# A three-part decoder layer on one core: row totals of both norms summed by VectorE's additions, squares about the mean summed by ScalarE

## What is computed

```
def _layernorm(x, axis=-1, eps=1e-05):
    m = jnp.mean(x, axis=axis, keepdims=True)
    v = jnp.var(x, axis=axis, keepdims=True)
    return (x - m) / jnp.sqrt(v + eps)
...
    x = _layernorm(x + _L0_attn_ref(x, ...), axis=-1)
    x = _layernorm(x + _L0_xattn_ref(ctx_1024, x, ...), axis=-1)
    x = _layernorm(x + _L0_ffn_ref(x, ...), axis=-1)
    return x
```

## Time and profile before

| | |
|---|---|
| runs | 1366.23 us median of 3 (1363.86 to 1369.6) |
| the profiled execution | 1370.82 us, of which the span of the instructions is 1368.9 us |
| PE busy | 1144.9 us (84%) |
| DVE busy | 1100.1 us (80%) |
| POOL busy | 997.2 us (73%) |
| ACT busy | 852.6 us (62%) |
| mean granted clock of PE | 0.88 of full speed |
| first scan, last scan | 51.95 us, 756.3 us |
| experts' first load of the slot table lands | about 820 us |

### The profile page before, as it was taken

How to read it: one execution, slowest core, us unless ns; L and a number is a source line. 1 busy time by engine, 2 the same in 40 slices (tenths; PEclk the granted TensorE clock), 3 DMA queues, 4 the chain that set the end, 5 groups by cost and what they waited for, 6 DMA issues and landing times. The chain is left out here.

```text
span 1368.9 us, 19497 instructions
## 1 busy us (share of the span) xinstructions
PE 1144.9 (84%) x6481; PEld 768.9 (56%) x6481; DVE 1100.1 (80%) x1534; ACT 852.6 (62%) x1536; POOL 997.2 (73%) x788
## 2 busy tenths in 40 slices
PE   7489997898968889978987536999999999999950
PEld 2234433353324544333533326999899999999950
DVE  2379988989968699778899354988889888989946
ACT  5474584734855445756354225888888888888843
POOL 0778778867999887999989703777777777777744
PEclk9688997899979689977998557999999999999985
DMA  6535326322252412163131208999999999999978
GB/s 239 136 74 193 103 64 154 108 56 72 49 139 57 129 51 64 34 152 108 31 81 32 62 17 277 267 305 303 308 301 303 307 307 307 303 314 304 302 130 331
DMA packets 97491, 235.26 MB, mean 172 GB/s; under 512 B 20705, under 2 KB 21217, under 8 KB 96753
## 3 DMA queue, kind: packets, MB, share of 16 engines
q1 hardware_dynamic: 65648, 162.66, 39.1%
q0 software_dynamic: 31744, 71.37, 21.8%
HBM read 147.48 MB, written 52.94 MB: 146 GB/s over the span
## 5 line engine op out<-in xcount | busy, mean ns | idle before, releaser
L1189 DVE TENSOR_TENSOR_SCAN hst<-hst,dbu 128x512 f32<-128x512 f32 x256 | 299.2, 1214 | 98.8 <-POOL dbu L1005 72.9
L1005 POOL TENSOR_TENSOR dbu<-rep,bc 128x1024 f32<-128x1024 f32 x128 | 301.8, 2359 | 67.1 <-PE y_ps L377 36.1
L1600 POOL DMA_INDIRECT sum_rows<-ye,tokens x128 | 205.5, 1605 | 101.0 <-ACT ye L1679 73.9
L377 PE MATMUL y_ps<-dbu,cs 128*32 128x512 f32 x512 | 158.0, 701 | 74.7 <-DVE dbu L1195 63.5
L1592 POOL DMA_INDIRECT xe<-x_rows,tokens x128 | 148.9, 1163 | 83.6 <-issue 37.8
L771 ACT ACTIVATE hst<-rep,small_sb 128x512 f32<-128x512 f32 x256 | 165.9, 685 | 47.7 <-DVE dbu L1195 42.1
L415 PE MATMUL ring<-wqkv,xT 128*128 128x512 f32 x384 | 178.7, 609 | 0.3 <-DVE x2T L1277 0.2
L1195 DVE TENSOR_TENSOR dbu<-hst,bc 128x1024 f32<-128x1024 f32 x128 | 156.7, 1225 | 4.4
L1642 PE MATMUL low<-xh,w1h 128*128 128x256 f32 x512 | 150.8, 295 | 0.7 <-DVE w1l L1753 0.7
L1642 PE MATMUL low<-xl,w1h 128*128 128x256 f32 x512 | 145.6, 284 | 0.0
L1642 PE MATMUL low<-xh,w1l 128*128 128x256 f32 x512 | 145.5, 284 | 0.0
(11 more groups left out here) (190 smaller groups left out, 2705.6 us busy)
## 6 DMA issues: line engine op xcount, KB each, us to landing
w<-in_gate_up SPq DMA_DIRECT2D x64, 768.0 KB
rep<-made SPq DMA_DIRECT2D x256, 128.0 KB
w<-in_down SPq DMA_DIRECT2D x64, 256.0 KB
bc<-bc_rows SPq DMA_DIRECT2D x64, 128.0 KB, 2.9
w<-in_down SPq DMA_DIRECT2D x64, 128.0 KB
rows<-sum_rows SPq DMA_DIRECT2D x16, 512.0 KB, 9.3
sum_rows<-x2T SPq DMA_DIRECT2D x1, 4608.0 KB, 16.7
xT<-in_x_turned SPq DMA_DIRECT2D x16, 256.0 KB, 3.0
```

The costliest lines, as they stand in the source:

```text
L377: ins = pe.matmul(y_ps[rows, :], sel, dbu[:, n % WORK, g, :], start=(k == 0), stop=(k == QUADS - 1))
L1005: pool.tensor_tensor(dbu[:, n % WORK, :, :], rep[:, i % 2, :, 1, :], bc[:, k, 0, :].unsqueeze(1).broadcast_to([P, 2, T]), ALU.mult).then_i ...
L1189: dve.tensor_tensor_scan(h, h, dbu[:, n % WORK, i, :], 0.0, ALU.mult, ALU.add).then_inc(scanned, 1)
L1600: pool.indirect_dma_start(sum_dram[e % SUMS], bass.IndirectOffsetOnAxis(ap=tokens[:, e, j:j + 1], axis=0), ye[:, e % YE, j, :], None, comp ...
```

## The change

Means and variances of both norms are no longer made with bn_stats and bn_aggr.

- DVE's addition, `scalar_tensor_tensor`, writes the row totals beside its result (total, total2). The second sum was a `tensor_tensor` and is now a `scalar_tensor_tensor` with a factor of 1.
- ACT has a new `center(t)`: the total times -1/512, which is the negative mean, and after a wait for it a Square of x1 with that as bias, whose row sums go to power. Its full output goes to a buffer that nobody reads. `center(t)` stands after decays(n + 8), ahead of the last excess or steps and of qT and kT. `center2(b, j)` does it for x2, four in a row, in tile c = 0 between taking v and decays(n + 8), and in the tail.
- POOL's roots take power times 1/512, plus eps; shift is the negative mean times rstd. `last_root` has one operation less. `norm_root(t - 1)` moves from k = 0, behind the first dbu product, to k = 1, behind everything that is done there.

```diff
+            def center(t):
+                c = t % NT
+                taken(act, f"wo{t}")
+                act.activation(total[:, c:c + 1], total[:, c:c + 1], ACT.Copy, scale=-1.0 / D).then_inc(centered, 1)
+                act.wait_ge(centered, t + 1)
+                act.activation(square_out[:, :], x1[:, c, :], ACT.Square, bias=total[:, c:c + 1],
+                               accum_out=power[:, c:c + 1]).then_inc(stats_ready, 1)
+
+            def center2(b, j):
+                taken(act, f"yT{b}_{j}")
+                act.activation(total2[:, j:j + 1], total2[:, j:j + 1], ACT.Copy, scale=-1.0 / D).then_inc(centered2, 1)
+                act.wait_ge(centered2, NT * b + j + 1)
+                act.activation(square_out[:, :], x2[:, j, :], ACT.Square, bias=total2[:, j:j + 1],
+                               accum_out=power2[:, j:j + 1]).then_inc(stats2_ready, 1)
...
+                    if back and c == 0:
+                        for j in range(NT):
+                            center2(b - 1, j)
                     if more:
                         decays(n + 8)
+                    center(t)
...
             def norm_root(t):
                 c = slice(t % NT, t % NT + 1)
                 pool.wait_ge(stats_ready, t + 1)
-                root(rstd[:, c], mv[:, t % NT, 1:2])
-                pool.tensor_scalar(shift[:, c], mv[:, t % NT, 0:1], rstd[:, c], -1.0, ALU.mult, ALU.mult).then_inc(rstd_ready, 1)
+                root(rstd[:, c], power[:, c], scale=1.0 / D)
+                pool.tensor_tensor(shift[:, c], total[:, c], rstd[:, c], ALU.mult).then_inc(rstd_ready, 1)
...
-                        if k == 0 and t:
-                            norm_root(t - 1)
...
                         if k in (3, 4) and c == 1:
                             steps_of_u(b, k - 1)
+                        if k == 1 and t:
+                            norm_root(t - 1)
...
                 dve.scalar_tensor_tensor(out=x1[:, c, :], in0=full(dve, f"wo{t}")[:, :], scalar=rms[:, c:c + 1],
-                                         in1=x_in[:, t % 2, :], op0=ALU.mult, op1=ALU.add).then_inc(drain_sem(f"wo{t}"), 1)
-                taken(dve, f"wo{t}")
-                own.step(dve.bn_stats(st[:, c, :], x1[:, c, :]))
-                own.settle()
-                dve.bn_aggr(mv[:, c, :], st[:, c, :]).then_inc(stats_ready, 1)
-                assert own.n == NORM_STEPS
+                                         in1=x_in[:, t % 2, :], op0=ALU.mult, op1=ALU.add,
+                                         accum_out=total[:, c:c + 1]).then_inc(drain_sem(f"wo{t}"), 1)
...
-                dve.tensor_tensor(x2[:, j, :], full(dve, use)[:, :], x1[:, j, :], ALU.add).then_inc(drain_sem(use), 1)
-                taken(dve, use)
-                own.step(dve.bn_stats(st2[:, j, :], x2[:, j, :]))
...
+                dve.scalar_tensor_tensor(out=x2[:, j, :], in0=full(dve, use)[:, :], scalar=1.0, in1=x1[:, j, :],
+                                         op0=ALU.mult, op1=ALU.add, accum_out=total2[:, j:j + 1]).then_inc(drain_sem(use), 1)
```

More of the change, by code:

```diff
@@ L84 @@
 TURN_STEPS = 3
-NORM_STEPS = 1
-NORM2_STEPS = NT
 ROUTE_STEPS = 25
@@ L186, in mixers @@
         rms = sb("rms", [P, NT])
-        st = sb("st", [P, NT, 6])
-        mv = sb("mv", [P, NT, 2])
+        total = sb("total", [P, NT])
+        power = sb("power", [P, NT])
+        square_out = sb("square_out", [P, D], F16)
         rstd = sb("rstd", [P, NT])
         shift = sb("shift1", [P, NT])
-        st2 = sb("st2", [P, NT, 6])
-        mv2 = sb("mv2", [P, NT, 2])
+        total2 = sb("total2", [P, NT])
+        power2 = sb("power2", [P, NT])
         rstd2 = sb("rstd2", [P, NT])
@@ L277, in mixers @@
         squared = sem("squared")
-        norm_steps = sem("norm_steps")
+        centered = sem("centered")
+        centered2 = sem("centered2")
         x1_ready = sem("x1_ready")
@@ L982, in _ @@
             gate_z(B - 1, 3)
+            for j in range(NT):
+                center2(B - 1, j)
             second_norm(B - 1)
@@ L1029, in _, with root @@
             roots = Chain(pool, root_steps)
-            def root(dst, src, done=None):
-                roots.step(pool.tensor_scalar(dst, src, 1.0, EPS, ALU.mult, ALU.add))
+            def root(dst, src, done=None, scale=1.0):
+                roots.step(pool.tensor_scalar(dst, src, scale, EPS, ALU.mult, ALU.add))
                 roots.settle()
@@ L1047, in norm_root @@
                 pool.wait_ge(stats_ready, t + 1)
-                root(rstd[:, c], mv[:, t % NT, 1:2])
-                pool.tensor_scalar(shift[:, c], mv[:, t % NT, 0:1], rstd[:, c], -1.0, ALU.mult, ALU.mult).then_inc(rstd_ready, 1)
+                root(rstd[:, c], power[:, c], scale=1.0 / D)
+                pool.tensor_tensor(shift[:, c], total[:, c], rstd[:, c], ALU.mult).then_inc(rstd_ready, 1)
             def last_root(b):
                 pool.wait_ge(stats2_ready, NT * (b + 1))
-                roots.step(pool.tensor_scalar(shift2[:, :], mv2[:, :, 0], -1.0, None, ALU.mult))
-                root(rstd2[:, :], mv2[:, :, 1])
-                pool.tensor_tensor(shift2[:, :], shift2[:, :], rstd2[:, :], ALU.mult).then_inc(rstd2_ready, 1)
+                root(rstd2[:, :], power2[:, :], scale=1.0 / D)
+                pool.tensor_tensor(shift2[:, :], total2[:, :], rstd2[:, :], ALU.mult).then_inc(rstd2_ready, 1)
             def rotate(t):
@@ L1418, in _ @@
                     if back and c == 0:
-                        second_sum(b - 1, chain["norm"], 2)
-                        second_sum(b - 1, chain["norm"], 3)
+                        second_sum(b - 1, 2)
+                        second_sum(b - 1, 3)
                     if front:
@@ L1425, in _ @@
                     add_attention(t)
-                    if back and c == 0:
-                        second_stats(b - 1, chain["norm"])
                     if back and c == 1:
```

18 lines of the change are left out of this document (4 added, 14 removed).

## The result

| | kernel before | changed kernel |
|---|---|---|
| median of the runs | 1365.55 us (6 runs, 1363.55 to 1369.6) | 1377.76 us (6 runs, 1374.64 to 1381.67) |
| ratio, 95% interval | | 1.0083 [1.0062, 1.0105] |
| profiled execution | 1370.82 us, span 1368.9 | 1380.38 us, span 1378.5 |
| first scan, last scan | 51.95, 756.32 us | 48.80, 768.67 us |

The change makes the kernel 0.83% slower, 11.3 us [8.5, 14.3]. The forecast was slower by 6.1 us. In the profiled executions the changed kernel takes 719.9 us from the first scan to the last instead of 704.4; what stands ahead is 3.1 us shorter and what stands behind 2.8. Both differ by as much between executions of kernels that are the same there (over the 14 profiled executions of this document the first scan starts at 48.80 to 51.95 us). So the loss is in the mixers, and single profiled executions give its size only roughly.

What follows compares the result with a forecast made beforehand. No engine bounds the mixers all the way; TensorE, DVE, and waits for ACT or POOL alternate. Losses 2.6 + 2.6 + 2.3 + 1.9 + 0.1 less gains 2.3 and 1.1 gave 6.1 us slower, 1372.3 us; range 1360 to 1382.

Steps and rivals of the forecast that it cites:

- The late root: Moving norm_root on POOL delays ACT's first_norm: 2.6 + 2.6 + 2.3 + 1.9 us lost in tiles 9, 5, 13 and 2.
- the wait of 1.9: Tile 2, ahead of the first convolution: the tap on ACT ends late and TensorE waits, 1.9 us lost.
- The terms for tiles 9 and 13: Ahead of the logits there, the mixed tile comes late behind first_norm: 2.6 us lost in tile 9, 2.3 in tile 13.
- that for tile 5: Tile 5, ahead of the logits: same order as tile 9, 0.8 from last_root nearly all taken up, 2.6 us lost.
- it goes through: Tile 9's mixed tile, 2.6 us late, delays the logits by as much, since TensorE is full after them.
- The rival that the clock falls: TensorE's stretch behind the logits falls to the lower clock in one tile: 1378.7 us if half, 1385.0 if all; chance 0.2.
- The centers: On ACT, 0.9 us each, hidden except 0.8 us passed down POOL's queue through last_root in batch 1.
- the term for c = 0: Four centers, 3.6 us, ahead of decays(n + 8); scan 40 starts some 2 us later, which tile 5's first half takes up.
- DVE's savings: Dropped statistics on DVE gain 2.3 us at the ends of tiles 5, 9 and 13 and 1.1 us in the tail.
- DVE paces c = 0 too: Tiles 4, 8 and 12 each give back 3.8 us, making the kernel faster, put at 1356 us; chance 0.12.
- The late root is absorbed: The logits wait for something else, so only the gains stay: -3.4 us, 1362.8 us; chance 0.13.
- It does not do what it says: Reading ACT's accumulator empties the engine, a center costs 1.5 us, tiles 5, 9, 13 lose more: 1376.7 us; chance 0.05.

Runs made afterwards that it cites:

- the root ahead in k = 1: The changed kernel with norm_root at k = 1 right behind the dbu product, ahead of decay_queries, decay_state and soft_rest: 1366.77 us, ratio 1.0009 to the kernel before.
- the added transposes: The kernel before with only norm_root moved to the end of k = 1, plus 16 more transposes in each of batches 0 to 2: 1381.55 us, ratio 1.0113.

## Why the prediction was right, and by what it was short

The sign and the place were right: slower, and through the root that passes soft_rest on POOL. The size was not: 11.3 us against 6.1.

- **The late root, 9.4 us forecast.** In the changed kernel it costs 0.0088 of the time, 12.0 us (1.0083 against 0.9995; 10.1 against the root ahead in k = 1, 1.0009); alone, 21.9. In tile 2 the wait of 1.9 was right: step k = 2 is 1.8 us longer. But the tile is 3.5 us longer, for behind the wait stand products at a lower granted clock. The terms for tiles 9 and 13, 2.6 and 2.3, measured 7.5 and 7.6 against the root put back; that for tile 5, 2.6, measured 0.4, where the centers make DVE late too. With the root moved alone, against the kernel before as the sum has it, tiles 2, 5, 9 and 13 are 3.6, 6.9, 4.6 and 7.6 us longer. In c = 3, priced at 0, it cost 0.7 us each in tiles 3 and 7: their step k = 4 takes 7.7 and 7.8 us instead of 7.1, as it does with the root moved alone, and 7.1 with all centers and the root ahead in k = 1. The step that failed is "it goes through": the mixed tile's lateness was passed on as so many microseconds of wait, with the logits behind it at their former duration. From the first logit product to the end of the last, tile 13 took 4.65 us before and 6.80 now (662.01 to 668.81), tile 9 6.62 and 8.06.
- **The rival that the clock falls**, chance 0.2 and 1378.7 us, is what happened beside the sum (measured 1377.8); that even the number fits is luck. It was priced in one tile and in the stretch behind the logits. It came in tile 13 and mostly in its logits, to a lesser part in tile 2, and in tile 9 the last sixteen products were at the lower clock before already. The argument against it, tile 5's full clock, holds for tile 5 alone. That all three tiles ran low with the root moved alone, and that work put into tile 5's wait brought its clock back, speaks against chance; but the wait just ahead does not decide it alone (last section).
- **The centers, 0.8 us forecast.** Alone they cost 4.6 us [1.8, 7.5]. Each was priced rightly (0.94). What was not is the term for c = 0: the decays that are 3.8 us late lengthen the last step of tiles 4, 8 and 12 by 2.5, 2.0 and 2.0 us and these tiles by 2.0, 1.4 and 1.2, where tile 8 was to keep its length. With the centers behind the decays the last step is as short as before. In tiles 9 and 13 the first step gives 1.6 back.
- **DVE's savings, 3.4 us forecast**, came to 5.3 with an uncertainty of 3.7: not contradicted. But the reason was too simple. In tile 5 the 0.78 us gave nothing (below), and the doubled statistics lengthened the step k = 6 of tiles 5 and 9 by 0.3 us each, not by 0.69, and that of tile 13 not at all.
- **DVE paces c = 0 too** (chance 0.12): no. The waits of the earlier trace rows grew by 0.9 and 2.3 us, and the full stretch is as full as before.
- **The late root is absorbed** (0.13): no. **It does not do what it says** (0.05): no, a center is 0.94 us.
- The Trainium skill ("VectorE: DVE Perf Modes", section "Two Vector instructions with no wait between them") had an operation with accumulator output as two instructions. The trace agrees: a DVE_READ_ACCUMULATOR of 82 ns stands behind each. It costs the next operation nothing that shows: in tile 5 of the kernel with the root put back, read and next operation both start at 306.25.

## What to carry over

When a step moves behind others on its engine, find the wait on the consumer's engine that it used to fill: lateness is free up to the end of that wait and costs in full behind it, here, in c = 1, at soft_rest. Where the late result ends at TensorE, price the products behind the wait at both clocks; with the root moved alone tiles 5, 9 and 13 had 1.9 to 3.5 us more idle time ahead of the logits and were 4.6 to 7.6 us longer. Before a difference of one tile is put down to an edit, look for the same tile in a kernel that shares the program up to there: 1.4 us of tile 2 were chance. And a cost or a gain that one kernel shows need not be there in its neighbour: the centers cost 4.6 us by themselves and hid 10 us of the late root.

## What the runs showed of the hardware

**An operation of DVE that waits inside itself for POOL.** `find_slots` adds chosen to prev, 64 columns (L1312 before, L1319 in the changed kernel, L1316 with the statistics doubled). It took 0.22 to 0.28 us with the statistics doubled and up to 2.47 us elsewhere, with no wait shown in front. DVE and POOL in tile 5, in the kernel before (first fence), with the root put back (second) and with the statistics doubled (third):

```profile
304.15 0.53 DVE L1312 TENSOR_TENSOR prev<-prev,chosen 128x64 f32<-128x64 f32 x1
...
302.24 2.36 POOL L1005 TENSOR_TENSOR dbu<-rep,bc 128x1024 f32<-128x1024 f32 x1 [1.86 <-PE y_ps L377]
```

```profile
307.62 1.47 DVE L1319 TENSOR_TENSOR prev<-prev,chosen 128x64 f32<-128x64 f32 x1
...
306.66 2.35 POOL L1025 TENSOR_TENSOR dbu<-rep,bc 128x1024 f32<-128x1024 f32 x1 [1.87 <-PE y_ps L376]
```

```profile
304.48 0.23 DVE L1316 TENSOR_TENSOR prev<-prev,chosen 128x64 f32<-128x64 f32 x1
```

POOL's product ends at 304.60 and 309.01, and DVE's small sum, at 304.68 and 309.09, 0.08 us behind it both times; in the third POOL's product had ended at 304.34, before the sum began. The operation stands 42 times in the 14 profiled executions, in tiles 5, 9 and 13: all 33 that overlap this product of POOL end 0.08 or 0.09 us behind it and take 0.52 to 2.47 us, and the other nine take 0.22 to 0.28. DVE came 0.9 us earlier in the second, against POOL, and lost it in this one operation: the summed busy time hides a wait, and tile 5's step k = 6 is 8.3 us long in both kernels. In tile 9 of the changed kernel another of these operations is held (timelines of DVE and POOL):

```profile
498.75 3.12 DVE L1321 TENSOR_TENSOR x2T<-x2T 128x256 f32<-128x256 f32 x1
...
499.22 2.36 POOL L1025 TENSOR_TENSOR dbu<-rep,bc 128x1024 f32<-128x1024 f32 x1
```

It takes 0.41 us otherwise. The Trainium skill ("SBUF — State Buffer", section "Who interferes with whom") says that a DVE instruction with two inputs in SBUF and a GpSimd instruction that reads SBUF share a read port, which one of them holds to its end while the other waits. The traces agree with it in the 33 overlaps. The last place fits only in part: DVE's operation is shown as begun before POOL's and still ended 0.29 us after it (501.87 and 501.58), so there the one that began first is the one that waited.

**TensorE's clock and its idle time ahead of the logits.** In the three tiles of the kernel with the root moved alone (2.64, 4.35 and 4.73 us idle) the last sixteen products took 3.51 us each, and 2.02 us in all nine tiles of three other kernels (the root put back; the root at k = 1 ahead of soft_rest in either kernel), behind 0.76 to 1.84 us of idle time. But the wait just ahead is not all that counts. They took 3.52 us behind 1.20 us in tile 9 of the kernel before, and as much behind 1.21 us in tile 13 with the root back and the centers behind the decays, and behind 1.61 us in tile 5 with the root late and the centers behind. In that last kernel tile 9 went the other way (timeline of PE):

```profile
475.45 1.17 PE L508 MATMUL ring<-small_sb,x2T 128*128 128x64 f32 x8 [3.56 <-ACT x2T L745]
...
477.26 1.81 PE L508 MATMUL ring<-small_sb,x2T 128*128 128x64 f32 x8
...
479.72 2.02 PE L508 MATMUL ring<-small_sb,x2T 128*128 128x64 f32 x16
```

Behind 3.56 us of idle time the second eight products ran at the lower clock (1.81 us; 1.00 in tile 5 with the added transposes) and the last sixteen at the upper; tile 13 did the same behind 3.58 us. So every wait of 2.37 us and more ahead of the logits was followed by the lower clock somewhere in them, shorter ones only in some tiles, and how many products it slowed differed from tile to tile. What else decides it stays open.
